# Relational graph layer: the copy in interleaved 4 KB runs, 120 early gathers at a memset beat, sums kept in the rows

## The reference, cut to what matters

```python
h = max(layernorm(x), 0)                       # row by row
deg = segment_sum(1, src); norm = rsqrt(deg[src]) * rsqrt(deg[dst])   # 0 where deg is 0
msg[e] = sum_b comps[type[e], b] * (h[dst[e]] @ bases[b]) * alpha[type[e]] * norm[e]   # 4 bases of 128x128
out = x + segment_sum(msg, src)                # added at row src[e]
```

## Time and profile before

| | us |
|---|---|
| median of 3 runs | 745.38 |
| profiled execution | 752.15 |
| its span, first to last instruction | 750.2 |
| VectorE busy | 596.4 (80%) |
| TensorE matmul busy | 574.7 (77%) |
| GpSimd busy | 540.3 (72%) |
| ScalarE busy | 370.1 (49%) |
| granted TensorE clock, mean | 0.927 |

### The profile page before, as it was taken

One profiled execution on the slowest core, in us unless ns is written; L12 is line 12 of the kernel. 1 busy time (PEld: TensorE's weight loads), 2 busy tenths in 40 slices (PEclk: granted clock), 3 DMA queues, 4 the chain that ended last, 5 costly groups with the idle time before them and its releaser, 6 DMA issues.

```text
span 750.2 us, 13642 instructions
## 1 busy us (share of the span) xinstructions
PE 574.7 (77%) x3922; PEld 406.0 (54%) x3922; DVE 596.4 (80%) x2624; ACT 370.1 (49%) x1494; POOL 540.3 (72%) x404
## 2 busy tenths in 40 slices
PE   4999985665676876987778788886797878888860
PEld 4666654443454645655556565655565656665430
DVE  7999995466775676886987899986998999998730
ACT  0345542244424678664545655645656534446530
POOL 3788886455555587778788888878878767767775
PEclk9999998687788899999998999999999999999995
DMA  8999999989833335444535455444455545544332
GB/s 272 287 326 339 331 361 323 319 296 327 307 101 81 70 54 122 79 92 69 109 52 100 92 86 95 96 81 95 82 95 96 92 78 78 86 57 82 35 36 25
DMA packets 56574, 108.89 MB, mean 145 GB/s; under 512 B 9339, under 2 KB 48264, under 8 KB 55684
## 3 DMA queue, kind: packets, MB, share of 16 engines
q0 software_dynamic: 34496, 25.72, 25.6%
q1 hardware_dynamic: 4416, 50.68, 18.7%
q10 hardware_dynamic: 17588, 31.62, 13.5%
HBM read 94.89 MB, written 64.61 MB: 213 GB/s over the span
## 4 chain that ended last, share of the span: by engine, by line
DVE 14%; DMA 13%; issue 10%; PE 9%; POOL 8%; ACT 7%; ACTq 0%; POOLq 0%
DMA out_dram<-acc,scatter_idx 11%; POOL out_dram L393 6%; DVE masked L481 4%; DVE part_sum L518 4%; PE pst L756 3%; PE pst L737 3%; DVE turned_hot L475 2%; POOL rows L372 2%; DVE same L537 2%; ACT acc L651 2%; DMA rows<-in_x_dram,dst_i 2%; DVE rows L518 2%; ACT scratch L603 2%; PE pst L764 1%; ACT scratch L595 1%
## 5 line engine op out<-in xcount | busy, mean ns | idle before, releaser
L393 POOL DMA_INDIRECT out_dram<-acc,scatter_idx x196 | 313.8, 1601 | 106.3 <-issue 53.7
L372 POOL DMA_INDIRECT rows<-in_x_dram,dst_i x196 | 224.4, 1145 | 96.4 <-issue 36.2
L737 PE MATMUL pst<-table_bits,turned_hot 128*128 128x198 f16 x1568 | 183.1, 267 | 84.0 <-DVE masked L481 61.1
L756 PE MATMUL pst<-bases_sb,h_turned 128*128 128x512 f32 x392 | 214.1, 629 | 0.0
L737 PEld LDWEIGHTS pst<-table_bits,turned_hot 128*128 128x128 f16 x1568 | 147.3, 105 | 113.6 <-issue 59.1
L518 DVE SCALAR_TENSOR_TENSOR part_sum<-pst,coef,part_sum 128x128 f32<-128x128 f32 x392 | 115.7, 343 | 96.2 <-ACT part_sum L641 89.3
L764 PEld LDWEIGHTS pst<-rows,same 128*128 128x128 f32 x392 | 73.0, 199 | 166.2 <-issue 152.1
L641 ACT ACTIVATE part_sum<-pst,coef 128x128 f32<-128x128 f32 x196 | 71.2, 363 | 183.4 <-PE pst L756 132.3
L481 DVE SCALAR_TENSOR_TENSOR masked<-iota_h,lo,pst 128x198 f32<-128x198 f16 x392 | 141.9, 415 | 20.9 <-PE pst L737 16.3
L764 PE MATMUL pst<-rows,same 128*128 128x128 f32 x392 | 82.7, 294 | 58.4 <-ACT acc L651 57.4
L651 ACT ACTIVATE acc<-pst,sum_scale 128x128 f32<-128x128 f32 x196 | 71.5, 365 | 58.5 <-DMA out_dram<-acc,scatter_idx 28.9
(11 more groups left out here) (71 smaller groups left out, 415.8 us busy)
## 6 DMA issues: line engine op xcount, KB each, us to landing
out_dram<-in_x_dram SPq DMA_DIRECT2D x46, 1000.0 KB
src_row<-src_rows ACTq DMA_DIRECT2D x25, 512.0 KB
edge_row<-edge_rows ACTq DMA_DIRECT2D x45, 256.0 KB
out_dram<-in_x_dram ACTq DMA_DIRECT2D x4, 1000.0 KB
rows<-in_x_dram,dst_i POOLq DMA_INDIRECT x196
out_dram<-acc,scatter_idx POOLq DMA_INDIRECT x196
rows<-edge_rows ACTq DMA_DIRECT2D x10, 175.0 KB
edge_row<-edge_rows SPq DMA_DIRECT2D x4, 256.0 KB
```

Source lines behind the costliest of these rows:

```text
L372: pool.indirect_dma_start(row(t), None, x, bass.IndirectOffsetOnAxis(ap=dst_i[:, t:t + 1], axis=0)) \
L393: pool.indirect_dma_start(out, bass.IndirectOffsetOnAxis(ap=scatter_idx[:, t:t + 1], axis=0), acc[:, t % ACC_RING, :], None, compute_op=AL ...
L737: last = pe.matmul(pst[:, LOOK + t % 2, k * LO:(k + 1) * LO], turned_hot[:, g % 2, c, k * W + j * P:k * W + (j + 1) * P], table[:, c * LO: ...
L756: pe.matmul(pst[:, PRODUCT + t % 4, :], h_turned[:, g % 2, j, :], bases_sb[:].rearrange("d b f -> d (b f)"), start=True, stop=True).then_i ...
```

## The change

Four things change.

1. The copies are 48 pieces of 2,048 rows and a last one of 1,696. Two pieces share a stretch of 4,096 rows: the even one takes the even runs of 8 rows (4,096 bytes), the odd one the odd runs, 256 runs each. Runs of one piece are therefore never neighbours in memory. As before, two pieces are under way at a time.
2. 120 gathers are issued ahead of the first scatter. The first 56 are paced by the histogram as before; each of the 64 others is preceded by two memsets of 128x40 on GpSimd, and GpSimd waits for each of them. Afterwards one gather stands ahead of every second scatter (76 left, up to scatter 152; before, 88 at 0.7 per scatter).
3. `keep_sum` writes the sum into `row(t)`, from which `add_same` and the scatter read it. The ring `acc`, and with it ScalarE's wait for scatter t - 6, is gone.
4. `edge_row` has five places. SyncE loads five ahead of the copies, and a load waits for the comparison of five groups back.

```diff
--- before.py
+++ after.py
@@ -62,12 +62,11 @@
     TYPE_AT = [TILES - 1 - (TYPE_TILES - 1) * (TYPE_PARTS - 1 - i) for i in range(TYPE_PARTS)]
     TW = TYPE_TILES * P
 
-    EDGE_RING = 4
+    EDGE_RING = 5
     HOT_RING = 6
     TYPE_RING = 4
     SAME_RING = 3 * BATCH
     PART_RING = 7
-    ACC_RING = 6
 
 
     def look_until(step):
@@ -80,14 +79,11 @@
 
     SUM_STEP, SUM_RATE = 3, 5
 
-
-    HIST_GATHERS = 56
-    LOOK_GATHERS = HIST_GATHERS + 4 * FIRST_LOOK * GROUP // 3
-    FIRST_GATHERS = LOOK_GATHERS + 3 * GROUP * SUM_STEP
+    HIST_GATHERS, FIRST_GATHERS = 56, 120
 
 
     def gathers_until(t):
-        return min(TILES, FIRST_GATHERS + (7 * t + 9) // 10)
+        return min(TILES, FIRST_GATHERS + t // 2)
 
     def sums_until(step):
         return min(TILES, GROUP * max(0, step), max(0, step - SUM_STEP + 1) * SUM_RATE)
@@ -110,12 +106,16 @@
         a, b = sums_until(step - 1), sums_until(step)
         return list(range(a + (b - a) * j // GROUP, a + (b - a) * (j + 1) // GROUP))
 
-    COPIES = 50
-    COPY_ROWS = N // COPIES
+
+
+    RUN_ROWS, RUNS = 8, 256
     COPY_RING = 2
+    PAIR_ROWS = 2 * RUNS * RUN_ROWS
+    COPIES = 2 * (N // PAIR_ROWS) + 1
+    LAST_COPY = (COPIES // 2) * PAIR_ROWS
 
     FIRST_COPIES = 4
-    assert COPIES * COPY_ROWS == N and COPIES % COPY_RING == 0
+    assert LAST_COPY < N and (N - LAST_COPY) * D % 32 == 0
 
     rows16_dram = nc.dram_tensor("edge_rows", (3, TILES * P), F16, kind="Internal").ap()
     src32_dram = nc.dram_tensor("src_rows", (TILES * P,), I32, kind="Internal").ap()
@@ -208,7 +208,7 @@
         carried = sb("carried", [P, 2, BATCH])
         sum_scale = sb("sum_scale", [P, TILES])
         scatter_idx = sb("scatter_idx", [P, TILES], I32)
-        acc = sb("acc", [P, ACC_RING, D])
+        beat = sb("beat", [P, 40])
 
         pst = ctx.enter_context(nc.psum_tensor("pst", [P, 8, BANK], F32))
         LOOK, TURNED, SUMS, PRODUCT = 0, 2, 3, 4
@@ -229,6 +229,7 @@
         row_table_ready = sem("row_table_ready")
         rows_stored = sem("rows_stored")
         idx_ready = sem("idx_ready")
+        beat_ended = sem("beat_ended")
         type_row_loaded = [sem(f"type_row_loaded{b}") for b in range(TYPE_RING)]
         edge_row_loaded = [sem(f"edge_row_loaded{r}") for r in range(EDGE_RING)]
         src_row_loaded = [sem(f"src_row_loaded{b}") for b in range(2)]
@@ -299,10 +300,18 @@
         def copy(engine, i):
             if i >= COPY_RING:
                 engine.wait_ge(copied[i % COPY_RING], 16 * (i // COPY_RING))
-            a = i * COPY_ROWS
-            flat_out, flat_x = (y[a:a + COPY_ROWS, :].rearrange("r d -> (r d)") for y in (out, x))
-            engine.dma_start(flat_out.rearrange("(q e) -> q e", q=32), flat_x.rearrange("(q e) -> q e", q=32)) \
-                .then_inc(copied[i % COPY_RING], 16)
+            if i < COPIES - 1:
+                a = i // 2 * PAIR_ROWS
+                to, of = (y[a:a + PAIR_ROWS, :].rearrange("(q s r) d -> s q (r d)", s=2, r=RUN_ROWS)[i % 2]
+                          for y in (out, x))
+            else:
+                to, of = (y[LAST_COPY:N, :].rearrange("r d -> (r d)").rearrange("(q e) -> q e", q=32)
+                          for y in (out, x))
+            engine.dma_start(to, of).then_inc(copied[i % COPY_RING], 16)
+
+        def copies_done(engine):
+            for b in range(COPY_RING):
+                engine.wait_ge(copied[b], 16 * len(range(b, COPIES, COPY_RING)))
 
         block = ctx.enter_context(nc.Block())
 
@@ -331,8 +340,7 @@
                 copy(sp, i)
 
             sp.wait_ge(spare_filled, 16)
-            for b in range(COPY_RING):
-                sp.wait_ge(copied[b], 16 * (COPIES // COPY_RING))
+            copies_done(sp)
             for b in range(2):
                 sp.wait_ge(scattered[b], 16 * HALF)
 
@@ -350,17 +358,16 @@
             pool.affine_select(out=later[:, 0:P], in_=later[:, 0:P], compare_op=ALU.is_ge, fill=0.0, base=0,
                                pattern=[[1, P]], channel_multiplier=-1).then_inc(ident_ready, 1)
 
+            beats = [0]
+
             def pace(t):
                 if 0 < t < HIST_GATHERS:
                     pool.wait_ge(hot_used, t * TILES // HIST_GATHERS)
-                elif HIST_GATHERS <= t < LOOK_GATHERS:
-                    pool.wait_ge(look_ps, (t - HIST_GATHERS) * FIRST_LOOK * GROUP // (LOOK_GATHERS - HIST_GATHERS) + 1)
-                elif LOOK_GATHERS <= t < FIRST_GATHERS:
-                    tile, part = divmod(t - LOOK_GATHERS, 3)
-                    if part == 0:
-                        pool.wait_ge(product_ready, tile + 1)
-                    else:
-                        pool.wait_ge(look_ps, FIRST_LOOK * GROUP + 2 * tile + part)
+                elif HIST_GATHERS <= t < FIRST_GATHERS:
+                    for _ in range(2):
+                        beats[0] += 1
+                        pool.memset(beat[:], 0.0).then_inc(beat_ended, 1)
+                        pool.wait_ge(beat_ended, beats[0])
 
             def gather(t):
                 g = t // GROUP
@@ -379,8 +386,7 @@
             gathered = FIRST_GATHERS
 
             pool.wait_ge(spare_filled, 16)
-            for b in range(COPY_RING):
-                pool.wait_ge(copied[b], 16 * (COPIES // COPY_RING))
+            copies_done(pool)
             for t in range(TILES):
                 for u in range(gathered, gathers_until(t)):
                     gather(u)
@@ -391,7 +397,7 @@
                     pool.wait_ge(scattered[t % 2], 16 * (t // 2))
                 pool.wait_ge(acc_ready, t + 1)
                 pool.indirect_dma_start(out, bass.IndirectOffsetOnAxis(ap=scatter_idx[:, t:t + 1], axis=0),
-                                        acc[:, t % ACC_RING, :], None, compute_op=ALU.add) \
+                                        row(t), None, compute_op=ALU.add) \
                     .then_inc(scattered[t % 2], 16)
 
         @block.vector
@@ -645,10 +651,7 @@
                 if t % BATCH == 0:
                     act.wait_ge(scatter_ready, t // BATCH + 1)
                 act.wait_ge(sums_ps, t + 1)
-                if t >= ACC_RING:
-                    u = t - ACC_RING
-                    act.wait_ge(scattered[u % 2], 16 * (u // 2 + 1))
-                act.activation(acc[:, t % ACC_RING, :], pst[:, SUMS, 0:D], ACT.Copy, scale=sum_scale[:, t:t + 1]) \
+                act.activation(row(t), pst[:, SUMS, 0:D], ACT.Copy, scale=sum_scale[:, t:t + 1]) \
                     .then_inc(acc_ready, 1)
 
             act.wait_ge(padded, 3)
@@ -764,7 +767,7 @@
                 last = pe.matmul(pst[:, SUMS, 0:D], same[:, t % SAME_RING, 0:P], row(t), start=True, stop=(t == 0))
                 if t >= 1:
                     last = pe.matmul(pst[:, SUMS, 0:D], same[:, (t - 1) % SAME_RING, P:2 * P],
-                                     acc[:, (t - 1) % ACC_RING, :], start=False, stop=True)
+                                     row(t - 1), start=False, stop=True)
                 last.then_inc(sums_ps, 1)
 
             pe.wait_ge(table_ready, CHUNKS)
```

## The result

The changed kernel takes 754.01 us, the median of four runs (752.2 to 757.27), beside 745.07 us (742.51 to 745.63, four runs) for the kernel before: ratio 1.0132, 95% interval 1.0086 to 1.0178. It is slower by 1.3%. I had forecast 719 us and given slower a chance of 0.07.

What follows compares the result with a forecast made beforehand. GpSimd was taken to bound steps 10 to 33, VectorE steps 34 to 39. Savings of 3.7 + 1.5 + 18.6 + 2.4 = 26 us gave span 724, profiled 726, less 6.8 for the median: 719 us, range 697 to 740.

Steps and rivals of the forecast that it cites:

- The rate of the pieces: The copy on SyncE's queue: 4 KB runs change nothing, 3.7 to 3.9 us per piece, landing at about 216.
- a rival for it: Short runs copy slowly, with engines' shares 128 KiB apart, and the kernel gets slower: above 745 us, chance 0.08.
- Where the rival would decide: First scatter at which a slow copy cancels the gain: 269, or 5.2 us a piece, 0.73 of the old rate.
- the price behind the first scatter: GpSimd from first scatter to end, never idle: 474.9 us of work plus 6.5 us of tail.
- Cover for a late first scatter: First scatter at 235 instead of 212.62 holds nobody up; GpSimd, 11 us late by 261, makes it good.
- The beat: 64 gathers ahead of the scatters, two waited memsets each at 0.30 us: 1.90 us per gather, through at 234.
- Small transfers: Smaller copy packets and a fifth edge row let loads land sooner: 3.7 us gained ahead of step 5, bounds 0 to 8.
- The steps: Steps 10 to 39 with fewer gathers: 10.7 us each, 321 us in all (309 to 338), 18.6 us less.
- Steps 5 to 9: Five steps bound by GpSimd, with fewer gathers: 65 us instead of 66.5, 1.5 us less (bounds 0 and 3.5).
- The end: From step 40 to the span's end, 90.4 us before: at most 7.4 us to gain, 2.4 taken.
- Sums in the rows: ScalarE's wait for scatter t - 6 goes, 21.4 us in the last stretch; 2.4 us of gain taken.
- From profile to median: The timed median stands 6.8 us below the profiled execution, so profiled 726 becomes 719.

Runs made afterwards that it cites:

- e2: The changed kernel with the old copy (50 pieces of 32 neighbouring runs of 32,000 bytes), other three parts kept: 731.16 us, ratio 0.9681 to the kernel before.
- e1: The copy alone, no layer: old pieces 169 us, interleaved 4 KB runs 215, the same with shares 120 KiB apart 221, 32 KB 166, four under way 172.
- e14: The copy alone, no layer, other distances: 162 us for every third 4 KB piece of memory, 186 for every fourth; with one under way 244 and 299.
- e15: The changed kernel with its 4 KB runs dealt to three pieces in turn instead of two (12 KB from start to start): 724.67 us, ratio 0.9637 to before.
- e12: The changed kernel with 8 KB runs, 132 gathers ahead of the first scatter and one memset each instead of two: 734.71 us, ratio 0.9872 to before.
- e10: The changed kernel with the old copy and without the memsets between gathers: 727.64 us, ratio 0.9788 to the kernel before.
- e9: The changed kernel with interleaved runs of 8 KB (128 of them) instead of 4 KB: 726.85 us, ratio 0.9798 to the kernel before.
- e4: The changed kernel with interleaved runs of 32 KB (64 rows, 32 runs) instead of 4 KB: 733.03 us, ratio 0.9719 to the kernel before.
- e7: The changed kernel with the old copy and the old order of gathers, with waits for TensorE in place of memsets: 751.03 us, ratio 0.9993 to before.
- e8: The changed kernel with the old copy, the ring acc of six and four edge rows again: 732.30 us, ratio 0.9727 to the kernel before.
- e11: The changed kernel with the old copy and the memsets, but 108 gathers ahead and 0.7 per scatter as before: 743.43 us, ratio 1.0002 to before.
- e5: The changed kernel with four pieces of the copy under way instead of two, runs still 4 KB: 741.16 us, ratio 0.9877 to the kernel before.
- e3: The kernel before with only the new copy in interleaved 4 KB runs: 771.92 us, ratio 1.0258 to the kernel before.
- e6: The copy alone, no layer: one under way 262 us (32,000 bytes) and 371 (4 KB); three under way 208; double pieces 191; 8 and 16 KB 163.
- e13: The copy alone, no layer, five loops: 4 KB base 216 us, even pieces first 227, 8 KB one under way 237, 2 KB 192, two queues about 214.

## Why the prediction was wrong, point by point

**The rate of the pieces** is the step that failed first. I put it at no change, because the bytes were the same and the DMA engines were already full; it is 4.74 us a piece instead of 3.83. It is 17.3 of the 26.3 us between the forecast span (724) and the measured one (750.3), as e2 with the old copy ends at 733.0. The gap in the argument: a share of 90% busy says that packets are under way, not at what rate they move. In the changed kernel the share went up (74.7% from 67.5%) and the bytes went down. I also misread: of its first eleven slices eight are at nine tenths and three at eight. I had a rival for it, with a chance of 0.08, but hung it on the wrong distance: on the 128 KiB between the engines' shares, where it was the 8 KB between the runs of a piece (e1, e14, e15). Of the rule in the Trainium skill (DMA: Bandwidth & Descriptors, Latency and other measured facts) my runs confirm only that distances in HBM can matter: 120 KiB between the shares was as slow as 128. No run here shows channels, which that section offers as an inference.

**Where the rival would decide.** The slow rate alone would not have made my forecast wrong: I allowed a first scatter up to 250 in it, and said that the rival decides from 269. The span was level with before at 249.2. This is the second step that failed, the price behind the first scatter: I counted 474.9 + 6.5 us for GpSimd never idle, which would have given 731, and measured were 501 (249.2 to 750.3). Scatters also waited for sums (12.6 us in 24 waits) and for each other (15.1 us in 20), and from step 12 on the steps themselves need 10.6 to 10.8 us (e12, e2), more than GpSimd's 10.29. That the loss came out in the rival's range (above 745) is so only because both errors pointed the same way.

**Cover for a late first scatter.** I wrote that ScalarE's first need for a late gather comes at step 8, and that GpSimd makes up for 11 us. It was 36.6 us late against before, and the cover ended at step 9: three waits of 6.4 to 9.6 us and two steps of 21 us. With a first scatter at 217 (e2) these waits are nearly gone, 2.2 us in all, and steps 10 and 11 take 19.9 us together.

**The beat.** Predicted 1.90 us from gather to gather and 234 for the last; measured 1.57 and 220.7. Two waited memsets cost about 0.30 us together (1.57 less the 1.26 of e10), not 0.60: in the trace they show as 0.34 us of GpSimd with a gap of 0.27 behind, beside the gap of 0.30 that a gather has anyway. My bound of 0.22 for one was too high.

**Small transfers.** Step 5 starts at 243.2, 10.4 us earlier; I had 3.7, with 8 as the bound. Of this, 4.2 us are an earlier start of step 0, which moves between 131.5 and 143.2 from run to run for no reason that I found. From step 0 to step 5 it is 107.0 us here, 105.1, 110.2 and 109.1 in e9, e12 and e15 with short packets, and 112 to 118 in the seven kernels with long packets (before, e2, e4, e7, e8, e10, e11); in e5, short packets with four pieces under way, 112.7. So the gain is likely and of about the size I gave, with one execution of each.

**The steps.** Steps 10 to 39 were predicted at 321 us; with the copy mended it is 320.4 (e2). Steps 5 to 9 were predicted at 65 and took 73.3 there, and this is 8.3 of the 9.0 us by which e2's span misses the forecast. They are not held by GpSimd (51.18 us of work and 37 gaps of 0.30, 62.3 in all). They hold nine groups of statistics with the new numbers of gathers, by `stats_until`, and eight with the old ones, and the times go with that: 66.2 to 68.3 us with eight (before, e3, e7, e11), 70.5 to 73.3 with nine (e2, e4, e5, e8, e9, e10, e15), 73.9 with ten (e12); the changed kernel, with nine and its late scatters, took 76.0. My sum had left this group out; that it is the cause was not tested by itself. The end was predicted at 88 and took 89.8. So the sum for the three other parts was 22.5 us (26 less the 3.7 ahead of step 5), and e2 shows 17.2 in the span and 3.2% in the timed runs.

**Sums in the rows**, for which I took 2.4 us: nothing measurable (e8).

**From profile to median.** I carried over that the median stands 6.8 us below the profiled execution. After, it stands 1.8 us above, which is 8.6 of the 35 us between 719 and 754. One profiled execution of several is no fixed distance from the median.

## What to carry to other kernels

A full DMA engine is not a fast one, as 74.7% of its time for 22.80 MB beside 67.5% for 26.50 shows: before the shape of a transfer is changed, look at bytes per busy share, and measure the copy alone in the new shape, which needs no layer around it. Where one engine's order mixes early work for others with its own late work, a late start of it is hidden only as far as the others are allowed to run ahead; count that distance in time before calling it cover. And what is taken off the bound pays only up to the next bound, here about 0.6 us of the 1.1 per step (339.6 / 30 less 320.4 / 30 in e2, against 11.36 less 10.29 of GpSimd's work).

## What the runs showed of the hardware

A copy from HBM to HBM in 1 MB pieces, two under way, nothing beside it, takes 169 us for 51.2 MB in pieces of 32 neighbouring runs of 32,000 bytes. For 50.3 MB it takes 166, 163 and 163 us in every second run of 32, 16 and 8 KB; 215 in every second run of 4 KB (216 when repeated in e13); 192 in every second run of 2 KB; 162 in every third run of 4 KB; 186 in every fourth; 159 in every third of 8 KB (e1, e6, e13, e14; each loop ran once). With one piece under way the spread is larger: 262, then 371 for every second run of 4 KB, 244 for every third, 299 for every fourth, 237 for every second of 8 KB, 293 for every second of 2 KB. Three under way left every second run of 4 KB at 208, four brought 172; pieces of twice the size, two under way, took 191. What has this pattern is open: one half of a 4 KB alternation would explain 8 and 12 KB, but not why 16 KB is better than 8. Nor did any loop have the distance on one side only, where it reads or where it writes.
